# Attention and group norm on one core: two more of eight tiles split, done on GpSimd, with scores four tiles ahead

## The chip, the cores and the metric

The kernel runs on one core of a Trainium2 chip. PE is TensorE, DVE is VectorE, ACT is ScalarE, POOL is GpSimd and SP is SyncE, which only issues DMAs here. The metric is the device time of one launch in microseconds.

## The reference

x is 8 images of 128 channels and 1024 pixels, f32. First an attention for each image, then a normalization over groups of four channels, the partners of each channel being the three that are the least correlated with it over all images.

```python
x_f = jnp.einsum('oc,bcn->bon', Wf, xf) + bf[None, :, None]     # 16 rows
x_g = jnp.einsum('oc,bcn->bon', Wg, xf) + bg[None, :, None]     # 16 rows
x_h = jnp.einsum('oc,bcn->bon', Wh, xf) + bh[None, :, None]     # 128 rows
s = jnp.einsum('bci,bcj->bij', x_f, x_g)
beta = jax.nn.softmax(s, axis=-1)
y = x + gamma[0] * jnp.einsum('bci,bij->bcj', x_h, beta)
x_n = y / jnp.maximum(jnp.linalg.norm(y, axis=2, keepdims=True), 1e-12)
cos = jnp.einsum('bcn,bdn->cd', x_n, x_n) / B
_, idx = jax.lax.top_k(-jnp.abs(cos).T, 4)
# mean and variance of each channel with its three partners, then scale and shift
```

## The kernel before

An image's 1024 pixels i are eight tiles t of 128 rows; all 1024 pixels j lie along the free dimension, in two halves of 512 (a PSUM bank each). All engines run the same list of slots: eight for each image b, one per attend of PE. `run_stages` (L212) writes out images 0, 1, 6 and 7 and loops over 2 to 5; each engine has a `stage` function of its own with what it does in slot t. The order on an engine is the order of its code, and semaphores counted up by each operation tie the engines together.

A tile goes through these steps: `score` (L617, PE) multiplies the parts of f and g into one of two PSUM buffers `s_ps`; `row_max` (L404, DVE) takes the negated maximum of 1024; `exp` (L318, ACT) writes `probs[t]` and the row sums; `invert_sum` (L408, DVE) takes the reciprocal; `scale_values` (L335, ACT) multiplies the tile's values by it; `attend` (L636, PE) adds values times probs onto `o_ps`. Tile t+3 is scored in slot t (AHEAD = 3), which waits for the exponential of tile t+1, since the two share a buffer. In plain f32 a product of 128x128 by 128x512 is two PE instructions. The tiles of SPLIT, 3 and 7, are split instead: `high_part` (L324, ACT) rounds probs to the short format fp32r, `split_parts` (L415 to L421, DVE) makes the rest and the two parts of the values, and three short products take the place of the f32 one. The high part is made in the slot before its low part.

f and g come from one projection (`project_fg`, L606, PE) with both weights four times over, 64 rows each. ACT copies it to SBUF with the bias (`copy_fg`, L308) and makes a negated rounded copy in the rows masked as low parts (L311); the sum of the two is the parts of g (`parts`, L427, DVE) and f (`parts_f`, L266, POOL). This is done in slots 1 to 3 for the image ahead, behind the maxima and exponentials of those slots. The values are projected in slots 5 and 6 (`project_values`, L611) from a copy `x_cur`, and `add_value_bias` (L435, DVE) takes them out of PSUM.

At the image's end `residual` (L447, DVE) writes y; ACT squares it (L348), PE transposes it in the next image (L645) and multiplies it with itself (`gram`, L651); `high_yT` (L362, ACT) and `low_part` (L452, DVE) make the parts for it. POOL makes one over the norm (L282, L289), `scale_gram` (L460, L463, DVE) applies it, `turn_gram` (L657, PE) transposes, `add_gram` (L469, DVE) adds up. All of f, g, values, transposes and gram share one PSUM tensor `w_ps`. DMAs on SP copy x and y to and from `x_cur` and `y_cur`. After the last image come the selection of the partners, the statistics, and scale, shift and store of all images.

## Time and profile before

| | us |
|---|---|
| median of three runs (214.33 to 214.99) | 214.97 |
| span of the profiled execution | 211.9 |
| PE busy | 186.4 |
| DVE busy | 173.7 |
| ACT busy | 143.9 |
| POOL busy | 34.3 |

Busy time is the union of an engine's instructions; they overlap a little at their ends, so what counts for a chain is the distance from one start to the next. The profile is one execution; the time of the runs is some 3 us more than its span. A row of the chain names the engine, the tensor written, the line and how many instructions in a row.

### The profile page before, as it was taken

How to read it: one execution, taken by the hardware profiler on the slowest of the kernel's cores; microseconds unless marked ns; L12 is line 12 of the kernel's file. 1: busy time of each engine (PE TensorE's matmuls, PEld its weight loads, DVE VectorE, ACT ScalarE, POOL GpSimd, SP SyncE). 2: the span in 40 equal slices, each digit the busy share in tenths (PEclk: the TensorE clock that was granted, in tenths of full speed). 3: DMA queues.
4: the chain of work that ended last, by engine and by line, in shares of the span. 5: the costliest groups of instructions: out<-in, count | busy, mean ns of one | idle time of the engine just before them, and what ended most of it. 6: DMA issues, size and time to landing. Idle time of an engine off the chain costs nothing.

```text
span 211.9 us, 2596 instructions
## 1 busy us (share of the span) xinstructions
PE 186.4 (88%) x727; PEld 115.2 (54%) x727; DVE 173.7 (82%) x317; ACT 143.9 (68%) x256; POOL 34.3 (16%) x39
## 2 busy tenths in 40 slices
PE   7669979999999999999999999999999999983100
PEld 3435546465765676466756675657465756462000
DVE  6588989979898889979797979887988898766660
ACT  2548976799379955995499658984799378740320
POOL 0200210034003400160007100520034001001400
PEclk9999999999999999999999999999999999997555
DMA  6240002500060007000520052002200020000198
GB/s 207 89 162 0 0 0 100 203 0 0 39 257 3 0 0 292 6 0 3 205 94 0 0 186 111 0 0 99 99 0 0 3 99 0 0 0 0 53 403 336
DMA packets 4904, 16.16 MB, mean 76 GB/s; under 512 B 544, under 2 KB 672, under 8 KB 4896
## 3 DMA queue, kind: packets, MB, share of 16 engines
q1 hardware_dynamic: 4320, 14.68, 18.4%
q10 hardware_dynamic: 576, 1.38, 1.7%
q8 instruction: 4, 0.07, 0.1%
q14 instruction: 4, 0.03, 0.0%
HBM read 4.52 MB, written 4.19 MB: 41 GB/s over the span
## 4 chain that ended last, share of the span: by engine, by line
PE 71%; DVE 13%; ACT 6%; issue 5%; POOL 1%; DVEq 0%; ACTq 0%; POOLq 0%
PE o_ps L636 40%; PE s_ps L617 11%; PE w_ps L611 6%; PE w_ps L606 6%; DVE nmax L404 3%; PE w_ps L651 3%; ACT probs L318 3%; PE w_ps L645 2%; PE o_ps L603 2%; DVE y_all L596 1%; DVE probs_low L418 1%; DVE g_parts L427 1%; DVE y_cur L447 1%; ACT probs_high L324 1%; DVE values L435 1%
## 5 line engine op out<-in xcount | busy, mean ns | idle before, releaser
L318 ACT ACTIVATE probs<-s_ps,nmax 128x1024 f32<-128x1024 f32 x64 | 70.9, 1108 | 40.5 <-DVE nmax L404 40.5
L636 PE MATMUL o_ps<-probs,vnorm 128*128 128x512 f32 x192 | 90.2, 594 | 0.5 <-DVE y_cur L447 0.5
L404 DVE TENSOR_REDUCE nmax<-s_ps 128x1 f32<-128x1024 f32 x64 | 77.9, 1218 | 10.2 <-PE s_ps L617 9.8
L617 PE MATMUL s_ps<-g_parts,f_parts 128*128 128x512 f32 x128 | 51.6, 485 | 4.6 <-ACT probs L318 2.3
L636 PEld LDWEIGHTS o_ps<-probs,vnorm 128*128 128x128 f32 x192 | 35.3, 189 | 28.8 <-issue 23.2
L266 POOL TENSOR_TENSOR f_parts<-fg,fg_neg 64x512 fp32r<-64x512 f32 x14 | 24.0, 1713 | 122.1 <-ACT fg_neg L311 122.1
L617 PEld LDWEIGHTS s_ps<-g_parts,f_parts 128*128 128x128 f32 x128 | 21.2, 190 | 20.7 <-issue 14.0
L418 DVE TENSOR_TENSOR probs_low<-probs,probs_high 128x1024 fp32r<-128x1024 f32 x16 | 19.5, 1221 | 1.3 <-ACT probs_high L324 1.2
L427 DVE TENSOR_TENSOR g_parts<-fg,fg_neg 64x512 fp32r<-64x512 f32 x16 | 13.9, 871 | 6.6 <-ACT fg_neg L311 6.5
L335 ACT ACTIVATE vnorm<-values,rinv 128x128 f32<-128x128 f32 x48 | 18.8, 391 | 0.0
L611 PEld LDWEIGHTS w_ps<-wd,x_cur 128*128 128x128 f32 x112 | 14.7, 192 | 6.7 <-issue 6.7
L324 ACT ACTIVATE probs_high<-probs 128x1024 fp32r<-128x1024 f32 x16 | 16.8, 1048 | 0.0
L606 PE MATMUL w_ps<-x_all,wd 128*128 128x512 f32 (+1 forms) x32 | 16.7, 615 | 0.0
L611 PE MATMUL w_ps<-wd,x_cur 128*128 128x128 f32 x112 | 14.8, 275 | 0.0
L308 ACT ACTIVATE fg<-w_ps,wd 128x512 f32<-128x512 f32 x16 | 10.8, 676 | 3.2 <-PE w_ps L606 3.2
L636 PE MATMUL o_ps<-probs_high,v_high 128*128 128x512 f32 x32 | 12.7, 398 | 0.1
L636 PE MATMUL o_ps<-probs_high,v_low 128*128 128x512 f32 x32 | 12.6, 394 | 0.0
L636 PE MATMUL o_ps<-probs_low,v_high 128*128 128x512 f32 x32 | 12.5, 391 | 0.0
L318 ACT ACTIVATION_READ_ACCUMULATOR probs<-s_ps,nmax 128x1 f32 x64 | 12.4, 194 | 0.0
L311 ACT ACTIVATE fg_neg<-fg,wd 128x512 fp32r<-128x512 f32 x16 | 11.6, 722 | 0.5
L447 DVE SCALAR_TENSOR_TENSOR y_cur<-o_ps,wd,x_all 128x512 f32<-128x512 f32 x14 | 10.0, 749 | 2.0 <-PE o_ps L636 1.7
L452 DVE TENSOR_TENSOR yT<-w_ps,yT 128x512 fp32r<-128x512 f32 x14 | 9.5, 682 | 2.1 <-ACT yT L362 2.1
(90 smaller groups left out, 165.7 us busy)
## 6 DMA issues: line engine op xcount, KB each, us to landing
x_all<-x_dram SPq DMA_DIRECT2D x7, 512.0 KB, 4.0
x_cur<-x_all SPq DMA_DIRECT2D x7, 512.0 KB, 3.2
y_all<-y_cur SPq DMA_DIRECT2D x7, 512.0 KB, 2.9
out_dram<-y_all SPq DMA_DIRECT2D x5, 512.0 KB, 5.8
out_dram<-y_all ACTq DMA_DIRECT2D x2, 512.0 KB, 4.1
x_all<-x_dram SPq DMA_DIRECT2D x2, 256.0 KB, 3.7
out_dram<-y_all SPq DMA_DIRECT2D x2, 256.0 KB, 2.2
wd<-wide_dram ACTq DMA_DIRECT2D x1, 256.0 KB, 4.3
```

The costliest lines, as they stand in the source:

```text
L266: nc.gpsimd.tensor_tensor(f_parts[b % 2][0:KP, halves[h]], fg32[0:KP, halves[h]], fg_neg[0:KP, halves[h]].bitcast(F32), ALU.add).then_inc( ...
L318: nc.scalar.activation(probs[t][:, :], s_ps[t % 2][:, :], ACT.Exp, bias=nmax[:, t:t + 1], accum_out=rsum[:, t:t + 1]).then_inc(exp_done, 1)
L324: nc.scalar.activation(probs_high[SPLIT.index(t)][:, :], probs[t][:, :], ACT.Copy).then_inc(high_ready, 1)
L335: nc.scalar.activation(vnorm[t][:, :], values[par][:, t, :], ACT.Copy, scale=rinv[:, t:t + 1]).then_inc(vn_ready, 1)
L404: nc.vector.reduce_max(nmax[:, t:t + 1], s_ps[t % 2][:, :], AX_X, negate=True).then_inc(max_ready, 1)
L418: nc.vector.tensor_tensor(probs_low[n][:, :], probs[t][:, :], probs_high[n][:, :].bitcast(F32), ALU.subtract).then_inc(low_ready, 1)
L427: nc.vector.tensor_tensor(to[0:KP, columns], fg32[rows, columns], fg_neg[rows, columns].bitcast(F32), ALU.add).then_inc(done, 1)
L447: nc.vector.scalar_tensor_tensor(y_cur[:, halves[h]], o_ps[:, halves[h]], wd[:, GAMMA:GAMMA + 1], image(x_all, b)[:, halves[h]], ALU.mult, ...
L606: return nc.tensor.matmul(w_ps[:, halves[h]], wd[:, WFG:WFG + P], image(x_all, b)[:, halves[h]], start=True, stop=True)
L611: last = nc.tensor.matmul(to[:, t * P:(t + 1) * P], source[:, t * P:(t + 1) * P], wd[:, WHT:WHT + P], start=True, stop=True)
L617: last = nc.tensor.matmul(s_ps[t % 2][:, h], f_parts[par][:, t * P:(t + 1) * P], g_parts[par][:, h], start=True, stop=True)
L636: last = nc.tensor.matmul(o_ps[:, halves[h]], weights[:, :], rows[:, halves[h]], start=(t == 0 and n == 0), stop=(t == T - 1 and n == len( ...
```

## The change

AHEAD goes from 3 to 4, and SPLIT from (3, 7) to (0, 2, 4, 5). For tiles 0 and 4 ACT makes the high part of the probabilities, already scaled by the reciprocal, and DVE the low one; for tiles 2 and 5 POOL does all: scale, high part, low part. The two parts of the values are no longer scaled and are made by POOL for two tiles at a time, as soon as the value bias is added. The copy of f and g to SBUF goes away: ACT makes the negated rounded copy straight from PSUM, and DVE adds PSUM, bias and that copy for f and g together in one operation of 128 rows; a DMA on SP moves g's 64 rows to the partitions of f (for image 0 DVE writes them there itself). The loop is written out, `x_cur`, `y_cur` and `y_all` and their DMAs go: y is written over x. In slots 0 and 1 the copy and the parts stand ahead of that slot's exponential and maximum. High part and low part of a vector-split tile are in the same slot. The value projections are in slots 4 and 5, the transposes in 2 and 3, the gram in slot 6, its scaling in slot 7 ahead of the residual. The diff, cut to this:

```diff
-AHEAD = 3
-SCALED = 2
-SPLIT = (3, 7)
+AHEAD = 4
+VECTOR_SPLIT = (0, 4)
+POOL_SPLIT = (2, 5)
+SPLIT = (0, 2, 4, 5)
...
+            for b in range(1, B):
+                for h in range(H):
+                    sp.wait_ge(parts_ready, H * b + h + 1)
+                    if b >= 2:
+                        sp.wait_ge(scores, T * (b - 1))
+                    sp.dma_start(g_low[b % 2][0:KP, halves[h]].bitcast(F32),
+                                 fg_parts[b % 2][KP:P, halves[h]].bitcast(F32)).then_inc(g_in[h], 16)
...
+            def split_values(b, h):
+                tiles = SPLIT_VALUES[h]
+                source = values[b % 2][:, tiles, :]
+                pool.wait_ge(v_ready, H * b + h + 1)
+                if b >= 2:
+                    pool.wait_ge(probs_used, T * (b - 1))
+                nc.gpsimd.tensor_copy(v_high[b % 2][:, tiles, :], source).then_inc(vh_ready, 1)
+                pool.wait_ge(vh_ready, H * b + h + 1)
+                nc.gpsimd.tensor_tensor(v_low[b % 2][:, tiles, :], source,
+                                        v_high[b % 2][:, tiles, :].bitcast(F32),
+                                        ALU.subtract).then_inc(vl_ready, 1)
+            def split_probs(b, t):
+                n, count = SPLIT.index(t), pool_split_count(b, t)
+                pool.wait_ge(rinv_ready, T * b + t + 1)
+                nc.gpsimd.tensor_scalar(probs[t][:, :], probs[t][:, :], rinv[:, t:t + 1], 1.0,
+                                        ALU.mult, ALU.mult).then_inc(pool_scaled, 1)
+                pool.wait_ge(pool_scaled, count)
+                nc.gpsimd.tensor_copy(probs_high[n][:, :], probs[t][:, :]).then_inc(pool_high, 1)
+                pool.wait_ge(pool_high, count)
+                nc.gpsimd.tensor_tensor(probs_low[n][:, :], probs[t][:, :], probs_high[n][:, :].bitcast(F32),
+                                        ALU.subtract).then_inc(pool_low, 1)
...
+            for b in range(B):
+                for t in range(T):
+                    its_b, its_t = ahead(b, t + AHEAD - 1)
+                    if b == 0 and t == 0:
+                        split_probs(0, 2)
+                    if its_b < B and its_t in POOL_SPLIT:
+                        split_probs(its_b, its_t)
+                    if t == 4 and b < L:
+                        split_values(b + 1, 0)
+                    if t == 5 and b < L:
+                        split_values(b + 1, 1)
+                    if t == 5 and b > 0:
+                        norm(b - 1)
+            norm(L)
             pool.wait_ge(table_in, 1)
...
+            def negate_high(b, h):
                 act.wait_ge(fg_proj, H * b + h + 1)
-                nc.scalar.activation(fg32[:, halves[h]], w_ps[:, halves[h]], ACT.Identity,
-                                     bias=wd[:, BFG:BFG + 1]).then_inc(fg_copied, 1)
-                act.wait_ge(fg_copied, H * b + h + 1)
-                nc.scalar.activation(fg_neg[:, halves[h]], fg32[:, halves[h]], ACT.Copy,
+                if b > 0:
+                    act.wait_ge(parts_ready, H * (b - 1) + h + 1)
+                nc.scalar.activation(fg_neg[:, halves[h]], w_ps[:, halves[h]], ACT.Identity, bias=bias_neg[:, 0:1],
                                      scale=wd[:, NMASK:NMASK + 1]).then_inc(neg_ready, 1)
...
+            def scale(b, t):
+                if t in POOL_SPLIT:
+                    return
                 act.wait_ge(rinv_ready, T * b + t + 1)
...
+                if t in VECTOR_SPLIT:
+                    nc.scalar.activation(probs_high[SPLIT.index(t)][:, :], probs[t][:, :], ACT.Copy,
+                                         scale=rinv[:, t:t + 1]).then_inc(high_ready, 1)
+                    return
+                act.wait_ge(v_ready, H * b + t // TH + 1)
+                nc.scalar.activation(vnorm[t][:, :], values[b % 2][:, t, :], ACT.Copy,
                                      scale=rinv[:, t:t + 1]).then_inc(vn_ready, 1)
...
+            for b in range(B):
                 for t in range(T):
...
+                    if b < L and t < H:
+                        negate_high(b + 1, t)
+                    nxt = ahead(b, t + AHEAD)
+                    if nxt[0] < B:
+                        exp(*nxt)
+                    nxt = ahead(b, t + AHEAD - 1)
+                    if nxt[0] < B:
+                        scale(*nxt)
+                    if b > 0 and t in (2, 3):
+                        high_yT(b - 1, t - 2)
+                    if b > 0 and t == 4:
+                        square(b - 1)
...
+            def low_part(b, t):
                 n = SPLIT.index(t)
...
+                dve.wait_ge(high_ready, vector_split_count(b, t))
+                nc.vector.scalar_tensor_tensor(probs_low[n][:, :], probs[t][:, :], rinv[:, t:t + 1],
+                                               probs_high[n][:, :].bitcast(F32), ALU.mult,
+                                               ALU.subtract).then_inc(low_ready, 1)
...
+            def parts(b, h):
+                dve.wait_ge(neg_ready, H * b + h + 1)
+                if b >= 2:
+                    dve.wait_ge(scores, T * (b - 1))
+                nc.vector.scalar_tensor_tensor(fg_parts[b % 2][:, halves[h]], w_ps[:, halves[h]], wd[:, BFG:BFG + 1],
+                                               fg_neg[:, halves[h]].bitcast(F32), ALU.add,
+                                               ALU.add).then_inc(parts_ready, 1)
...
+            def residual(b, h):
+                if h == 0:
+                    dve.wait_ge(first_half, b + 1)
+                else:
+                    dve.wait_ge(probs_used, T * (b + 1))
+                nc.vector.scalar_tensor_tensor(x_all[:, b, halves[h]], o_ps[:, halves[h]], wd[:, GAMMA:GAMMA + 1],
+                                               x_all[:, b, halves[h]], ALU.mult, ALU.add,
+                                               accum_out=sums[:, h, b:b + 1]).then_inc(y_ready, 1)
...
+            for b in range(B):
+                for t in range(T):
+                    if t == 0 and b >= 2:
+                        add_gram(b - 2, w_ps[:, BANK:BANK + P])
+                    if t < H and b < L:
+                        parts(b + 1, t)
+                    nxt = ahead(b, t + AHEAD)
+                    if nxt[0] < B:
+                        row_max(*nxt)
+                    nxt = ahead(b, t + AHEAD - 1)
+                    if nxt[0] < B:
+                        invert_sum(*nxt)
+                    if t == T - 1 and b >= 1:
+                        scale_gram(b - 1, w_ps)
+                    if t == T - 1:
+                        residual(b, 0)
+                        residual(b, 1)
+                    if nxt[0] < B and nxt[1] in VECTOR_SPLIT:
+                        low_part(*nxt)
+                    if b >= 1 and t in (3, 4):
+                        low_yT(b - 1, t - 3, w_ps[:, halves[t - 3]])
+                    if b < L and t in (5, 6):
+                        add_value_bias(b + 1, t - 5, w_ps)
+            for h in range(H):
...
+            def score(b, t):
+                if (b, t) != (0, 0) and (b, t) != (0, 1):
+                    pe.wait_ge(exp_done, T * b + t - 1)
+                if b > 0 and t == 0:
+                    for h in range(H):
+                        pe.wait_ge(g_in[h], 16 * b)
...
+            def attend(b, t):
                 if t in SPLIT:
-                    pe.wait_ge(vl_ready, split_count(b, t))
+                    pe.wait_ge(vl_ready, H * b + t // TH + 1)
+                    if t in POOL_SPLIT:
+                        pe.wait_ge(pool_low, pool_split_count(b, t))
+                    else:
+                        pe.wait_ge(low_ready, vector_split_count(b, t))
+                    n = SPLIT.index(t)
+                    high, low = v_high[b % 2][:, t, :], v_low[b % 2][:, t, :]
+                    products = [(high, probs_high[n]), (low, probs_high[n]), (high, probs_low[n])]
                 else:
                     pe.wait_ge(vn_ready, whole_count(b, t))
+                    products = [(vnorm[t][:, :], probs[t])]
...
+                    nxt = ahead(b, t + AHEAD)
+                    if nxt[0] < B:
+                        score(*nxt)
+                    if t == 0 and b < L:
+                        if b == 0:
+                            pe.wait_ge(x_in[1], 16)
+                            pe.wait_ge(parts_ready, H)
+                        else:
+                            pe.wait_ge(x_in[(b + 1) % 2], 16 * ((b + 1) // 2 + (b + 1) % 2))
+                        if b >= 2:
+                            pe.wait_ge(gram_scaled, b - 1)
+                        project_fg(b + 1, 0)
+                    if t == 0 and b >= 2:
+                        pe.wait_ge(v_ready, H * (b + 1))
+                        turn_gram(b - 2, w_ps[:, BANK:BANK + P])
+                    if t == 0 and b == 0:
+                        pe.wait_ge(v_ready, H)
+                    attend(b, t)
+                    if t == 1 and b < L:
+                        if b >= 2:
+                            pe.wait_ge(gram_added, b)
+                        elif b == 1:
+                            pe.wait_ge(v_ready, H * (b + 1))
+                        project_fg(b + 1, 1)
+                    if t in (2, 3) and b >= 1:
+                        h = t - 2
+                        if b < L:
+                            pe.wait_ge(parts_ready, H * (b + 1) + h + 1)
+                        elif h == 0:
+                            pe.wait_ge(gram_scaled, b - 1)
+                        else:
+                            pe.wait_ge(gram_added, b)
+                        transposes(b - 1, h, w_ps[:, halves[h]])
+                    if t in (4, 5) and b < L:
+                        h = t - 4
+                        if b >= 1:
+                            pe.wait_ge(yT_ready, H * (b - 1) + h + 1)
+                        else:
+                            pe.wait_ge(parts_ready, H * (b + 1) + h + 1)
+                        project_values(b + 1, h, w_ps)
+                    if t == 6 and b >= 1:
+                        pe.wait_ge(yT_ready, H * b)
+                        if b < L:
+                            pe.wait_ge(v_ready, H * (b + 1) + 1)
+                        gram(w_ps, range(T)).then_inc(gram_made, 1)
```

## Rows read from the trace of the kernel before

**Rows 1.** Windows, one image: stretch, then busy us of each engine, clock, DMA

```profile
104.23:126.46 22.23, 22.23 (x90) 14.00 (x90) 19.48 (x36) 17.26 (x31) 4.32 (x4) 1.00 0.20 74
```

**Rows 2.** The chain that ended last: start us, us on the chain, what

```profile
6.37 0.69 ACT fg L308
...
37.36 1.95 PE o_ps L636 x4
...
105.98 0.46 PE s_ps L617 x2
106.44 1.72 PE o_ps L636 x4
108.16 0.86 PE w_ps L606 x2
...
112.61 1.39 PE o_ps L636 x6
...
119.23 0.89 PE w_ps L611 x8
...
125.05 0.95 PE w_ps L651 x8
...
188.33 0.45 PE s_ps L645 x4
```

**Rows 3.** Timeline of PE: start us, us, first attend of images 0 and 7

```profile
16.53 1.88 PE L636 MATMUL o_ps<-probs,vnorm 128*128 128x512 f32 x4
...
170.95 1.88 PE L636 MATMUL o_ps<-probs,vnorm 128*128 128x512 f32 x4
```

**Rows 4.** Timeline: how operations follow one another on ACT and DVE

```profile
102.73 1.12 ACT L318 ACTIVATE probs<-s_ps,nmax 128x1024 f32<-128x1024 f32 x1 [1.26 <-DVE nmax L404]
103.74 0.19 ACT L318 ACTIVATION_READ_ACCUMULATOR probs<-s_ps,nmax 128x1 f32 x1
103.83 0.39 ACT L335 ACTIVATE vnorm<-values,rinv 128x128 f32<-128x128 f32 x1
...
106.97 1.21 DVE L404 TENSOR_REDUCE nmax<-s_ps 128x1 f32<-128x1024 f32 x1
108.10 0.15 DVE L408 RECIPROCAL rinv<-rsum 128x1 f32<-128x1 f32 x1
```

**Rows 5.** Groups by line and form: count, busy us, mean ns, idle before, releaser

```profile
L266 POOL TENSOR_TENSOR f_parts<-fg,fg_neg 64x512 fp32r<-64x512 f32 x14 | 24.0, 1713 | 122.1 <-ACT fg_neg L311 122.1
L418 DVE TENSOR_TENSOR probs_low<-probs,probs_high 128x1024 fp32r<-128x1024 f32 x16 | 19.5, 1221 | 1.3 <-ACT probs_high L324 1.2
L324 ACT ACTIVATE probs_high<-probs 128x1024 fp32r<-128x1024 f32 x16 | 16.8, 1048 | 0.0
L308 ACT ACTIVATE fg<-w_ps,wd 128x512 f32<-128x512 f32 x16 | 10.8, 676 | 3.2 <-PE w_ps L606 3.2
L447 DVE SCALAR_TENSOR_TENSOR y_cur<-o_ps,wd,x_all 128x512 f32<-128x512 f32 x14 | 10.0, 749 | 2.0 <-PE o_ps L636 1.7
L435 DVE TENSOR_TENSOR values<-w_ps,wd 128x512 f32<-128x512 f32 x14 | 9.4, 675 | 0.0
L289 POOL TENSOR_TENSOR rnorm<-nsq,mhalf 128x1 f32<-128x1 f32 x8 | 4.5, 568 | 0.7
L463 DVE SCALAR_TENSOR_TENSOR gram_rows<-w_ps,rnorm,gram_high 128x128 f32<-128x128 f32 x7 | 2.5, 351 | 0.2
L282 POOL TENSOR_SCALAR nsq<-stats 128x1 f32<-128x1 f32 x7 | 1.7, 242 | 14.3 <-ACT squares L348 14.3
```

**Rows 6.** Timeline, image 0: POOL's part of f and DVE's part of g

```profile
23.19 1.29 POOL L266 TENSOR_TENSOR f_parts<-fg,fg_neg 64x512 fp32r<-64x512 f32 x1 [12.65 <-ACT fg_neg L311]
...
23.43 1.59 DVE L427 TENSOR_TENSOR g_parts<-fg,fg_neg 64x512 fp32r<-64x512 f32 x1
```

**Rows 7.** DMA issues: count, KB each, median us from issue to landing

```profile
x_cur<-x_all SPq DMA_DIRECT2D x7, 512.0 KB, 3.2
```

**Rows 8.** Windows, ten us of the tail: columns as in group 1

```profile
190.00:200.00 10.00, 3.16 (x16) 2.10 (x16) 6.50 (x27) 1.37 (x3) 2.92 (x5) 0.68 0.00 0
```

430 lines of the change are left out of this document (131 added, 299 removed).

## The prediction

> **What bounds the kernel now.** I read the busy times of one whole image first, then the chain that ended last, then the order of the instructions on each engine. In the image from 104.23 to 126.46 us PE is busy all 22.23 us, VectorE 19.5, ScalarE 17.3, GpSimd 4.3 [rows 1]. So PE sets the pace. The chain agrees: from 37.36 us on it is PE after PE, and its pieces add up to the image [rows 2]: eight scores at 0.46, six plain attends at 1.72, two split attends at 1.39, two f/g projections at 0.86, two value projections at 0.89, two groups of transposes at 0.44, a gram at 0.95 and 0.10 for the turned gram: 22.2. The anchors of the sum are the first attend at 16.53, image 1's at 37.36, the last image's at 170.95, and the last transposes' end at 188.78 [rows 2, 3]. That is 16.5 of head, 20.8 for image 0, 133.6 for six images, 17.8 for the last, and 23.1 of tail to 211.9.
>
> **What the change gives PE.** Two more tiles of eight are split: 2 x (1.72 - 1.39) = 0.66 us less per image, so 21.55 of PE work. That is all PE gains; 8 images would make 5.3 us. It counts only while PE is still the one that is late.
>
> **What it costs to get a tile ready.** Durations as they follow each other on an engine [rows 4, 5]: a maximum takes 1.22 and the next VectorE operation starts after 1.14; an exponential is complete after 1.20 and the next ScalarE operation starts after 1.10; I take 0.05 for a handoff. High part 1.05, low part 1.22 (the new one has a scalar too: 1.22 taken, 1.3 at most), copy from PSUM 0.68, value bias 0.68, residual half 0.75. The new parts operation reads PSUM and SBUF: between the 0.68 of the value bias and the 0.75 of the residual; I take 0.70. Removed from VectorE are four small value operations and the g parts; it stays under 19.5 busy. ScalarE loses two copies and two value scalings and is no bound either. The removed copies of x and y on SP were hidden. The new DMA of g moves 128 KB; the nearest row is 512 KB in 3.2 us [rows 7], its upper end, and the lower is a quarter of that. It starts when the parts are there, and the score that needs it comes 7 us after that, as chain A below shows: hidden. Without that chain's stall the score would come 3.4 us after the parts (4.9 less the copy and the parts), still hidden by 0.2. The DMAs wait behind one another on SP and hold up the load of image b+2, which isn't read until an image later.
>
> **The order inside the queues is the point.** Each engine runs in order, so I write out what a waiting instruction holds up. Count slots t = 0 to 7 of image b, each one attend of PE. The score of slot t is that of tile t+4 and waits for the exponential of tile t+2.
>
> Chain A. PE does the projection of half 1 of the next image after the attend of slot 1. ScalarE in slot 1 has the negated copy ahead of the exponential of tile 5, VectorE has the parts ahead of the maximum of tile 5, though that tile's score was done two operations earlier. Then VectorE's low part of tile 4 waits for ScalarE's high part of tile 4, which stands behind the exponential of tile 5; and the maximum of tile 6 is queued behind that low part. From the end of the projection: handoff 0.10, negated copy 0.73, parts 0.62, maximum 1.27, exponential 1.11, high part 1.10, low part 1.17, maximum 1.27, exponential of tile 6 1.25 = 8.6 us until PE may do the score of slot 4. PE has only slots 2 and 3 in between: (0.46 + 1.39 + 0.44) + (0.46 + 1.72 + 0.44) = 4.9. PE stands 3.7 us per image. In the kernel before, maximum and exponential came ahead of the copies, and the high part was made a slot before its low part was due: there VectorE waited 1.2 us for high parts in the whole run (the idle column of L418 in [rows 5]).
>
> Chain B. From that same exponential on: high yT 0.64, low yT 0.61, maximum of the next image's tile 0 1.27, exponential 1.11, value scaling of tile 7 0.31, squares 1.14, exponential of tile 1 1.11, high part of tile 0 1.10, low part 1.17, value bias 0.61, maximum 1.14, reciprocal 0.08, value bias 0.73; then GpSimd splits these values (0.58 + 0.81, below), norm 0.30 + 0.62, then VectorE scales the gram 0.37 + 0.40, and only then may PE project f and g again. Sum 14.1, less 0.14 by which ScalarE was free before the exponential counted: 14.0. PE's own work over that stretch: 2.74 + 2.74 + 3.13 + 2.18 + 0.46 = 11.25. PE stands another 2.7 us.
>
> An image takes 21.55 + 3.7 + 2.7 = 28.0 us instead of 22.25.
>
> **GpSimd's prices.** No row shows its operations at this size. A two-input one of 64x512 took 1.29 where it began ahead of VectorE's, 1.71 in the mean, and one of 128x1 0.24 [rows 5, 6]. So (1.29 - 0.24)/512 = 2.05 ns per element with two inputs. I take half of that for one input, because two streams are read in the one and one in the other: 128x1024 costs 1.29, 1.29 and 2.34 for the scale, the high and the low part, 4.9 us per tile; 256 elements cost 0.50 and 0.76. The lower end is 0.24 for a one-input and 1.29 for a two-input operation, the upper end 2.34 for each of the three. GpSimd is then busy 2 x 4.9 + 2.5 + 0.9 = 13 us of 28. GpSimd has from the reciprocal in slot t-3 to slot t, 3 slots, less the 1.9 us in which VectorE gets to the reciprocal: 6.6 us (slots 7, 0 and 1), so hidden in the middle images by 1.6 us, and by more where PE stands. In the last image it isn't. The lower end shortens chain B by 0.8 and the last image by 3; the upper end gives 28.4 per image and 2.3 more in the last one. The Trainium skill (GPSIMD Engine Reference, Engine selection) says that elementwise work with one input runs there at roughly line rate, where two inputs take about twice VectorE's time; by its 1.2 GHz a one-input tile would be an estimated 0.85 us, and the whole time some 2 us below mine; no row here shows which.
> The trace shows a collision: VectorE's g parts took 1.59 us when GpSimd had begun 0.24 earlier [rows 6], where the value bias, of as many elements per partition, takes 0.68 [rows 5]. The remaining VectorE operation with two SBUF inputs is the low part; by chain A it runs at slots 1 to 2, when GpSimd is between two tiles, so I put it at nothing; at worst it waits 2.3 us for a GpSimd operation, once per image.
>
> **Head, image 0, last image, tail.** Head: one copy per half and the memsets leave; the first copy from PSUM starts at 6.37 as before [rows 2], and the g and f parts are four operations of 0.67 in a row on VectorE, from 7.1 to 9.8; then maximum, bias, maximum (11.5 to 12.8), exponential, high part, exponential to 16.1, score, projection: first attend at 17.4 (0.9 later). Image 0: both chains run without the gram: 26.3 instead of 20.8 (copies, parts, maxima and exponentials of tiles 3 to 6 from 16.2 to 31.1, PE's slot 4 to 33.9, then maximum, exponential, high part, low part, bias, maximum, bias, maximum, residual to 43.7). Last image: maxima, exponentials and low part up to the reciprocal of tile 5 take 8.3, GpSimd 5.0, then PE 1.39 + 1.72 + 0.95 + 1.88 and the residual 0.9: 20.3 instead of 17.8. Tail: the same steps, 23.1.
>
> **Sum.** 17.4 + 26.3 + 6 x 28.0 + 20.3 + 23.1 = 255.1, against a span of 211.9. Around the span lie 214.97 - 211.9 = 3.1 us, the median of the runs against the profiled one. Forecast 258.2 us.
>
> **Rivals.**
> (a) PE stays the bound, faster: its place is the score of slot 4, and it decides at 4.9 us: if the copies and parts don't hold up the maxima, PE never waits and the time is 214.97 - 5.3 = 209.7. For it: the kernel before has 2.7 us of free VectorE time in each image [rows 1] and the change cuts its operations. Against it: chain A is 8.6 and uses no unknown price. 0.04.
> (b) Chain A alone holds; B hides, because the norm or the value split is earlier than I put it: 25.3 per image and 2 off image 0: 240. For it: B has the many small terms. 0.11.
> (c) GpSimd becomes the bound: at 3 us and more for an operation (by the upper end it isn't yet) the tiles of slots 2 and 5 are late in each image: 265 to 285. For it: 1.71 in the mean where 1.29 was enough [rows 5, 6]. 0.09.
> (d) PE's granted clock falls in the stalls. From 190 to 200 us, where PE was busy 3.2 of 10 us, its mean was 0.68 [rows 8], between the two levels of 1.2 and 2.4 GHz; at half clock for 5 us of work after each stall of chain A it is 7 x 5 = 35 more: 293. Against it: the forecast keeps PE busy three quarters of the time, and its stalls come in pieces of 2 us. The Trainium skill (TensorE: Matmul & The Clock Gate, section HAM oscillation) names repeated waits between bursts of matmuls as what brings half clock, which speaks for this rival; no row here shows it for gaps of this size. 0.03.
> (e) The removed instructions and the new waits cancel: within 0.3%. 0.01.
>
> **Chances and range.** The forecast has 0.72; its bounds are 249 (GpSimd cheap) to 266 (GpSimd dear, low part 1.3, parts 0.75). To leave out no more than 2 in 10 the range takes in (b): 240 to 267. A measurement of this kernel can tell about 0.3% from no change. Faster 0.04, same 0.01, slower 0.95.
>
> **What would show it.** In the changed profile: images 28 us apart; PE busy about 77% in the middle; PE's scores waiting for the exponential, some 3.7 us over slots 3 and 4 (half of it at the score of tile 7, as its exponential is late as well); VectorE's low part waiting for the high part about 1.1 us each time; the maximum of tile 5 starting straight after the parts; the projection waiting for the scaled gram; split attends at 1.39; one-input GpSimd operations near 1.3. It is wrong if scores don't wait, if VectorE's maxima start as soon as the score is there, or if PE waits for GpSimd in the middle images.

## The result and the profile after

The changed kernel took 266.54 us (median of 4 runs, 265.83 to 269.53) beside 214.80 for the kernel before, run in turn with it: a ratio of 1.244, 95% interval 1.237 to 1.250. The forecast was 258.2 with a range of 240 to 267. The time is at the upper edge of the range (the ratio put on the 214.97 that the forecast started from makes it 267.4, just outside); the direction of the loss was right, the centre was 8.3 us too low. Ratios leave out the executions that were over 1.5% longer than the fastest of their kernel: one of the kernel before (259.92 us), and one each of three edited kernels below (277.17, 264.24 and 1085 us).

The page of the profile after, its first rows: busy time of each engine over a span of 264.7 us, the granted clock in 40 slices, and the chain that ended last by engine.

```profile
PE 198.4 (75%) x759; PEld 126.2 (48%) x759; DVE 162.3 (61%) x283; ACT 135.4 (51%) x231; POOL 101.7 (38%) x106
PEclk9858799999999999988999999979999999979655
DVE 31%; PE 27%; ACT 18%; issue 13%; POOL 7%; DVEq 0%; ACTq 0%; POOLq 0%
```

PE, which was busy through the whole image before [rows 1], is busy 75% of the span and makes up only 27% of the chain. VectorE and ScalarE with the time between them ("issue") make up the most. Windows of three neighbouring images and of two short stretches (columns as in group 1):

```profile
75.00:103.30 28.30, 22.75 (x94) 14.68 (x94) 18.90 (x31) 16.23 (x29) 12.14 (x13) 1.00 0.10 28
103.30:133.20 29.90, 24.14 (x94) 16.17 (x94) 18.89 (x31) 16.33 (x29) 12.14 (x13) 0.94 0.10 27
133.20:161.50 28.30, 22.74 (x95) 14.68 (x94) 18.87 (x31) 16.22 (x29) 12.13 (x13) 1.00 0.10 29
...
14.00:20.00 6.00, 5.00 (x9) 2.86 (x10) 3.53 (x7) 4.43 (x8) 2.89 (x3) 0.50 0.00 0
117.00:121.00 4.00, 4.00 (x16) 3.50 (x15) 2.49 (x4) 3.98 (x8) 2.94 (x2) 0.57 0.00 0
```

No engine is full: PE 22.7 of 28.3 us, VectorE 18.9, ScalarE 16.2, GpSimd 12.1. An image that no engine fills is set by the order in which they hand over. The middle image is 1.6 us longer than its neighbours, and its granted clock is 0.94: from 117.5 to about 121 it lay at the lower of its two levels, as it did in the head (the last two rows).

The waits of the whole run (engine and line, what it waited for: us in total, times, longest us):

```profile
DVE probs_low L396 <- ACT probs_high L316: 33.8, 16, 2.2
PE s_ps L593 <- ACT probs L307: 28.6, 18, 2.2
PE w_ps L570 <- DVE gram_rows L444: 5.2, 5, 1.0
PE o_ps L614 <- POOL probs_low L249: 4.2, 6, 3.0
```

VectorE waited 33.8 us for high parts, each time about 2.1, where it was 1.2 us in all before [rows 5]. PE's scores waited for exponentials, its projection for the scaled gram. For GpSimd's tiles PE waited 4.2 us in all: 3.0 of them once, in the last image, and 0.24 before the attend of tile 5 in five others, where the chain ran through ScalarE or VectorE and not through that attend.

Chain A in image 3, read from the chain that ended last (start us, us, what):

```profile
106.84 0.87 PE w_ps L570 x2
...
107.74 0.79 ACT fg_neg L300
...
108.55 0.75 DVE fg_parts L404
109.30 1.14 DVE nmax L387
...
111.67 1.05 ACT probs_high L316
...
112.75 1.28 DVE probs_low L396
114.03 1.15 DVE nmax L387
...
116.46 0.72 PE s_ps L593 x2
```

It is the chain that the prediction wrote out, link by link, from the projection's end at 107.71 to the score at 116.46. The timeline shows the two places where PE stood, and why the second followed the first (start us, us, instruction, in brackets the idle time before it and its releaser):

```profile
109.22 1.21 DVE L387 TENSOR_REDUCE nmax<-s_ps 128x1 f32<-128x1024 f32 x1
110.47 1.11 ACT L307 ACTIVATE probs<-s_ps,nmax 128x1024 f32<-128x1024 f32 x1 [1.95 <-DVE nmax L387]
111.73 0.73 PE L593 MATMUL s_ps<-g_low,fg_parts 128*128 128x512 f32 x2 [1.74 <-ACT probs L307]
112.75 1.28 DVE L396 SCALAR_TENSOR_TENSOR probs_low<-probs,rinv,probs_high 128x1024 fp32r<-128x1024 f32 x1 [2.24 <-ACT probs_high L316]
113.95 1.22 DVE L387 TENSOR_REDUCE nmax<-s_ps 128x1 f32<-128x1024 f32 x1
116.46 0.72 PE L593 MATMUL s_ps<-g_low,fg_parts 128*128 128x512 f32 x2 [1.84 <-ACT probs L307]
```

The maximum at 113.95 is of a tile whose score was ready; it stood behind the low part at 112.75, and that behind the high part at 111.67, and that behind the exponential at 110.47. The anchors, from the same chain: the head up to the first attend of image 0, then the first attends of images 1, 4 and 6 (those of 2, 3, 5 and 7 are at 74.98, 103.30, 161.53 and 219.23), and the attends of tiles 5 and 6 of the last image:

```profile
16.22 1.22 PE s_ps L593 x2
17.44 1.71 PE w_ps L570 x2
19.14 2.56 PE o_ps L614 x6
...
46.61 1.41 PE o_ps L614 x6
...
133.20 1.39 PE o_ps L614 x6
...
191.43 1.39 PE o_ps L614 x6
...
232.28 5.02 PE o_ps L614 x10
```

### The profile page after: what moved, and what is told of

Its sections match the earlier page's. It is cut to its first block, busy times and chain, and to the rows that moved or that the text cites. A ratio compares the mean times of both kernels' runs of the same rounds, so it can differ in the third digit from the quotient of the medians.

```text
span 264.7 us, 2435 instructions
## 1 busy us (share of the span) xinstructions
PE 198.4 (75%) x759; PEld 126.2 (48%) x759; DVE 162.3 (61%) x283; ACT 135.4 (51%) x231; POOL 101.7 (38%) x106
## 4 chain that ended last, share of the span: by engine, by line
DVE 31%; PE 27%; ACT 18%; issue 13%; POOL 7%; DVEq 0%; ACTq 0%; POOLq 0%
PE o_ps L614 13%; DVE nmax L387 12%; DVE probs_low L396 7%; ACT probs_high L316 6%; ACT probs L307 6%; PE w_ps L570 6%; PE s_ps L593 4%; DVE values L418 3%; ACT fg_neg L300 2%; DVE fg_parts L404 2%; POOL v_low L237 2%; ACT squares L325 2%; PE w_ps L575 2%; POOL rnorm L262 2%; PE o_ps L567 1%
## 5 line engine op out<-in xcount | busy, mean ns | idle before, releaser
L593 PE MATMUL s_ps<-g_low,fg_parts 128*128 128x512 f32 x128 | 50.9, 481 | 29.3 <-ACT probs L307 28.6
L614 PE MATMUL o_ps<-probs,vnorm 128*128 128x512 f32 x128 | 62.8, 614 | 0.0
L244 POOL TENSOR_SCALAR probs<-probs,rinv 128x1024 f32<-128x1024 f32 x16 | 18.0, 1123 | 74.3 <-DVE rinv L391 73.8
L593 PEld LDWEIGHTS s_ps<-g_low,fg_parts 128*128 128x128 f32 x128 | 22.3, 200 | 44.5 <-ACT probs L307 37.9
L396 DVE SCALAR_TENSOR_TENSOR probs_low<-probs,rinv,probs_high 128x1024 fp32r<-128x1024 f32 x16 | 20.6, 1285 | 33.8 <-ACT probs_high L316 33.8
L249 POOL TENSOR_TENSOR probs_low<-probs,probs_high 128x1024 fp32r<-128x1024 f32 x16 | 38.1, 2382 | 1.4
L404 DVE SCALAR_TENSOR_TENSOR fg_parts<-w_ps,wd,fg_neg 128x512 fp32r<-128x512 f32 x16 | 12.0, 751 | 23.8 <-ACT fg_neg L300 23.7
L614 PE MATMUL o_ps<-probs_high,v_low 128*128 128x512 f32 x64 | 26.3, 411 | 0.0
L570 PE MATMUL w_ps<-x_all,wd 128*128 128x512 f32 x32 | 17.6, 638 | 5.2 <-DVE gram_rows L444 5.2
L614 PEld LDWEIGHTS o_ps<-probs_high,v_high 128*128 128x128 f32 x64 | 12.5, 196 | 12.1 <-issue 9.7
L316 ACT ACTIVATE probs_high<-probs,rinv 128x1024 fp32r<-128x1024 f32 x16 | 18.2, 1138 | 0.0
L247 POOL CAST probs_high<-probs 128x1024 fp32r<-128x1024 f32 x16 | 16.6, 1041 | 1.0
L575 PEld LDWEIGHTS w_ps<-wd,x_all 128*128 128x128 f32 x112 | 16.4, 210 | 1.4
```

Of the source, the lines that this page charges most:

```text
L244: nc.gpsimd.tensor_scalar(probs[t][:, :], probs[t][:, :], rinv[:, t:t + 1], 1.0, ALU.mult, ALU.mult).then_inc(pool_scaled, 1)
L249: nc.gpsimd.tensor_tensor(probs_low[n][:, :], probs[t][:, :], probs_high[n][:, :].bitcast(F32), ALU.subtract).then_inc(pool_low, 1)
L316: nc.scalar.activation(probs_high[SPLIT.index(t)][:, :], probs[t][:, :], ACT.Copy, scale=rinv[:, t:t + 1]).then_inc(high_ready, 1)
L396: nc.vector.scalar_tensor_tensor(probs_low[n][:, :], probs[t][:, :], rinv[:, t:t + 1], probs_high[n][:, :].bitcast(F32), ALU.mult, ALU.sub ...
L404: nc.vector.scalar_tensor_tensor(fg_parts[b % 2][:, halves[h]], w_ps[:, halves[h]], wd[:, BFG:BFG + 1], fg_neg[:, halves[h]].bitcast(F32), ...
L570: nc.tensor.matmul(w_ps[:, halves[h]], wd[:, WFG:WFG + P], x_all[:, b, halves[h]], start=True, stop=True).then_inc(fg_proj, 1)
```

## The experiments

Theory T (the prediction's): the order inside the queues sets the time. VectorE's low part waits for a high part that ScalarE makes only behind the next exponential, and the next maximum is queued behind it; the copies and parts add their length at the worst moment. Rivals: G, GpSimd's load or its late norm; N, that what the trace shows as clock loss, or some price, carries it; and C, that the place of the copies and parts by itself is the cause. Each ratio below is to the kernel before, run beside it (214.6 to 214.9 us).

**The low part a slot later.** One line of VectorE's order:

```
-                    if nxt[0] < B and nxt[1] in VECTOR_SPLIT:
-                        low_part(*nxt)
+                    due = ahead(b, t + AHEAD - 2)
+                    if due[0] < B and due[1] in VECTOR_SPLIT:
+                        low_part(*due)
```

> The changed kernel, but VectorE makes the low part of tiles 0 and 4 one slot later (slots 6 and 2 in place of 5 and 1), so that the high part is there and the next maximum is not queued behind a wait for it. Theory (queue order, chains A and B): both chains lose the wait for exponential and high part; by the durations of the changed kernel's trace 24.9 us per image in place of 28.3, and 241 us in all. Rival 1 (the copies and parts ahead of the exponentials are the cause, not the high part): under 5 us gained, 262 or more. Rival 2 (GpSimd is the bound): no gain.

Measured: 237.04 us (236.03 to 238.04), ratio 1.104 [1.092, 1.116], 24.92 us per image. The waits of this kernel (columns as above):

```profile
DVE probs_low L396 <- ACT probs_high L316: 6.3, 8, 0.9
PE s_ps L594 <- ACT probs L307: 16.1, 10, 2.2
```

No instruction was removed, only one wait moved behind other work, and 29.5 us went. That is T: the image is as expected (24.9), and the whole is 4 us below the 241 expected, about what the lower clock had cost in images 3, 5 and 7 (below); in this kernel it stays at 1.00 there.

**GpSimd's norm ahead of its value splits.**

```
+                    if t == 4 and b > 0:
+                        norm(b - 1)
                     if t == 4 and b < L:
                         split_values(b + 1, 0)
...
-                    if t == 5 and b > 0:
-                        norm(b - 1)
```

> The changed kernel, but GpSimd makes one over the norm ahead of its two value splits (slot 4) instead of behind them (slot 5). Theory: the end of chain B (value bias, GpSimd's split 1.2 us, norm 0.9 us, scaled gram, projection) is cut by the value split and norm, 1.1 us per image (28.3 to 27.2), 260 us. Rival (b) of the prediction (chain B is covered anyway): no gain, 266.

Measured: 259.26 us, ratio 1.208 [1.200, 1.215], 27.23 us per image. The scaled gram no longer appears among the waits of the projection. So the end of chain B ran through VectorE's value bias, GpSimd's value split and its norm, and was worth 1.1 us per image. So much of G holds: not GpSimd's load, but the place of its norm in the chain.

**Copies and parts behind the exponentials and maxima.**

```
-                    if b < L and t < H:
-                        negate_high(b + 1, t)
                     nxt = ahead(b, t + AHEAD)
                     if nxt[0] < B:
                         exp(*nxt)
+                    if b < L and t < H:
+                        negate_high(b + 1, t)
```

(and in the same way `parts` behind `row_max` on VectorE.)

> The changed kernel, but in slots 0 and 1 the negated copy stands behind the exponential on ScalarE, and the parts behind the maximum on VectorE, as it was in the kernel before. If their place ahead is what costs, as chain A was told, 0.73 + 0.62 us per image go: 258. If the in-order wait for the high part is what costs, the same operations stand in the same cycle, only in another order (the low part then waits for copy and exponential and high part): 28.5 per image, 267.

Measured: two executions, of 266.13 and 277.17 us with mean clocks of 0.92 and 0.87, too far apart for a verdict; the shorter one is near the 267 expected and the 266.54 of the changed kernel. The window of one image of the longer one:

```profile
104.84:135.74 30.90, 25.20 (x94) 16.99 (x94) 18.91 (x32) 16.34 (x28) 12.13 (x13) 0.89 0.09 26
```

In the longer one the clock loss hides the edit's effect. It was repeated below with PE kept at work.

**No tiles on GpSimd, two split tiles of eight.**

```
-POOL_SPLIT = (2, 5)
-SPLIT = (0, 2, 4, 5)
+POOL_SPLIT = ()
+SPLIT = (0, 4)
...
```

(and GpSimd splits the values of these two tiles only.)

> The changed kernel with only tiles 0 and 4 split, tiles 2 and 5 plain f32; GpSimd then has only the value splits and the norm, PE has 0.66 us more work per image, and ScalarE scales two more tiles of values. Theory: neither PE nor GpSimd sets the pace in the middle, so the image stays within 0.5 of 28.3 us, and only the last image gains what it waited for GpSimd (3 us) less the PE work: 265 to 267. Rival (c) (GpSimd is the bound): 10 us or more off.

Measured: 262.04 us (260.95 to 263.12), ratio 1.221 [1.207, 1.234]. An image (columns as in group 1):

```profile
104.32:133.73 29.41, 24.81 (x90) 15.42 (x90) 18.90 (x32) 16.90 (x31) 2.25 (x6) 0.94 0.10 28
```

GpSimd's work falls from 12.1 to 2.3 us, and the image stays as long (28.08 at clock 1.00, this one of 29.41 at 0.94). G falls for the middle. The gain is 3 to 4.5 us, a little more than expected, and most of it lies in the end: from the last projection to the last transposes 48.1 us instead of 51.3, where nothing waits for GpSimd's tile 5 any more.

**PE kept at work in its stall.** Two matmuls more per image, whose results are overwritten by the transposes that follow; nothing that is computed changes.

```
+                        if h == 1:
+                            for _ in range(2):
+                                nc.tensor.matmul(w_ps[:, halves[h]], ident, x_all[:, b - 1, halves[h]],
+                                                 start=True, stop=True)
                         transposes(b - 1, h, w_ps[:, halves[h]])
```

> The changed kernel with two more matmuls of 128x512 f32 on PE in slot 3, ahead of the second transposes: 1.7 us of work whose result is overwritten, in a stretch in which PE stands anyway. Theory (the forecast missed by the clock): the granted clock stays at 1.00 in images 3 and 5, which fall from 29.9 to 28.3 us; with the last image's share the time falls by 3 to 5 us, to 262 or 263, although PE has more to do. Rival (the long images have another cause): no change or up to 2 us more per image.

Measured: 262.14 us (261.22 to 262.69), ratio 1.219 [1.215, 1.223]. The windows of images 3 and 4, and the attends of tiles 5 and 6 of the last image in the chain:

```profile
103.07:131.40 28.33, 24.54 (x98) 15.46 (x98) 18.90 (x32) 16.24 (x28) 12.15 (x13) 1.00 0.10 29
131.40:159.72 28.32, 24.50 (x97) 15.46 (x98) 18.91 (x32) 16.24 (x28) 12.12 (x13) 1.00 0.10 29
```

```profile
230.11 3.34 PE o_ps L614 x10
```

PE did 1.8 us more in each image, the middle images took 28.33, and the kernel became 4.4 us faster. The clock in these stalls cost 4.4 us of the 51.7 lost; with the head and image 0, which this edit does not mend and where the cost is read from rows, N carries a seventh of the loss (7.3 us, below).

**Place of the copies again, with PE kept at work** (the third edit and the fifth together).

> The copies-behind kernel again, with two matmuls of 128x512 in slot 3 of PE (results overwritten) that keep the clock up, to be set against the filled changed kernel (262.1 us, 28.3 per image), which has the same fill. Theory (the wait for the high part in the same slot holds the cycle, not the place of the copies): 28.2 to 28.8 us per image, 261 to 265. Rival (the copies ahead of the exponentials are what costs): 27.0 per image, 253.

Measured: 260.3 us, ratio 1.212 [1.210, 1.215]; 28.24 us per image where the filled kernel takes 28.33 (one image, at a lower clock, took 29.83). C falls for the middle images: with the low part where it is, the copies and parts may stand on either side of the exponentials and maxima. In image 0 their place does count: its score of slot 4 comes at 30.96 us instead of 33.06.

**Parts and value bias moved, the low part left.** PE filled as before; parts behind the maximum, in slots 0 and 2, and the bias in slots 4 and 5.

```
-                    if t < H and b < L:
-                        parts(b + 1, t)
...
+                    if t in (0, 2) and b < L:
+                        parts(b + 1, t // 2)
...
-                    if b < L and t in (5, 6):
-                        add_value_bias(b + 1, t - 5, w_ps)
+                    if b < L and t in (4, 5):
+                        add_value_bias(b + 1, t - 4, w_ps)
```

> The filled changed kernel with two of the three moves of the reordered one: parts behind the maximum in slots 0 and 2, value bias one slot earlier, but the low part left where the change has it. Theory: the low part is the larger share of the 6.2 us: here 26.9 us per image in place of 28.3, 252 us. Rival (parts and bias are the larger share): under 25 per image, 240.

Measured: 252.81 us (251.27 to 253.44), ratio 1.176 [1.171, 1.182], 26.47 us per image:

```profile
100.75:127.22 26.47, 24.17 (x98) 15.43 (x98) 18.44 (x32) 16.24 (x29) 12.17 (x13) 1.00 0.11 31
```

VectorE's wait for high parts even rose, to 46.3 us. 1.9 us per image come from the shorter chains, as expected within 0.5. That is a lower bound of what the two moves are worth: the two added matmuls, which stood off the chain in the filled kernel, stand on it here (chain that ended last):

```profile
112.47 1.98 PE w_ps L686 x4
```

They start only when the parts are there, and the score behind them comes at 114.81, though its exponential was complete at about 113.0; without them the moves may be worth up to 1.8 us more. So this run doesn't show that the low part is the larger share, and which of the two moves brings how much was not separated.

**All three orders at once** (low part a slot later, parts behind the maximum in slots 0 and 2, value bias in slots 4 and 5), without the fill.

> The changed kernel in another order, nothing added or taken away: low parts one slot later; the parts of f and g behind the maximum, in slots 0 and 2 instead of ahead of it in 0 and 1; the value bias one slot earlier, in 4 and 5. Theory: all waits of chains A and B are then shorter than PE's own work, and the image takes the 21.6 to 21.8 us of that work, which is 0.5 less than in the kernel before; with the head's 2.6 us more it is 213.5 us in all. Rival (splitting on GpSimd, the written-out code or the in-place y cost something of their own): 22.5 us per image or more, over 220.

Measured: 217.47 us (216.84 to 218.09), ratio 1.012 [1.009, 1.015]. PE's waits for exponentials are down to 3.5 us, from 28.6. The window of an image:

```profile
84.47:106.55 22.08, 22.03 (x94) 14.67 (x94) 18.94 (x32) 16.09 (x29) 13.92 (x13) 1.00 0.13 37
```

PE is busy 22.03 of 22.08 us again. Everything else of the change is still there: four split tiles, GpSimd, the DMA of g. So 49.1 of the 51.7 us went with the order of three operations, the clock loss of images 3, 5 and 7 among them, since the stalls in which it came are gone. What is left against the kernel before lies at the two ends. Per image it wins 0.17 (22.25 to 22.08), not the 0.66 of the sum: the first projection takes 1.03 instead of 0.86, and the attend of GpSimd's tile 5 takes 1.61 instead of 1.39, together 0.39 of the missing 0.49. That tile's last operation ends at 120.31 where the attend starts at 120.45, since the one before it (a cast, 1.04 elsewhere) took 1.90 beside VectorE's low part, so GpSimd is now just late enough to be felt:

```profile
120.45 1.61 PE o_ps L615 x6
```

```profile
115.93 1.90 POOL L247 CAST probs_high<-probs 128x1024 fp32r<-128x1024 f32 x1
117.92 2.39 POOL L249 TENSOR_TENSOR probs_low<-probs,probs_high 128x1024 fp32r<-128x1024 f32 x1
```

(The first line is of the chain, the others of GpSimd's timeline.) In the last image PE waits through the three operations of GpSimd (chain that ended last, start us, us, what):

```profile
179.16 2.17 POOL probs L244
...
181.38 1.05 POOL probs_high L247
...
182.50 2.38 POOL probs_low L249
...
185.01 3.32 PE o_ps L615 x10
```

**Head and end mended.** The same, with five matmuls to keep PE at work in the head (overwritten, as above), both projections of image 1 in slot 0, its parts in slots 0 and 1, and tile 5 of the last image unsplit.

```
+        def is_split(b, t):
+            return t in SPLIT and not (b == L and t == 5)
...
             for t in range(AHEAD):
+                if t >= 2:
+                    pe.wait_ge(parts_ready, H)
+                    keep_busy(2 if t == 2 else 1)
                 score(0, t)
+            keep_busy(2)
...
                         project_fg(b + 1, 0)
+                        if b == 0:
+                            project_fg(1, 1)
```

> The reordered kernel with its head and its last image mended: PE has five matmuls of 128x512 (results overwritten) in the waits before the first attends, both projections of image 1 stand in slot 0 with their parts in slots 0 and 1, and tile 5 of the last image is plain f32, so that PE doesn't wait for GpSimd there. By the reordered kernel's trace: the half clock of the head costs 1.7 us, the wait for the moved g in image 0 2.1 us, GpSimd's scale, high and low part of tile 5 after the last reciprocal 5.8 us, of which 3.5 can go. 217.5 - 7.3 = 210 us, 2% under the kernel before. Rival: another wait takes the place of each, and it stays at 215 or more.

Measured: 213.54 us, ratio 0.994 [0.992, 0.996]; 3.5 short of what was expected. The larger part is missing in the last image: from its first attend to the end of the last transposes it took 19.07 us in the reordered kernel and takes 17.72 here, so 1.35 of the 3.5 us came. PE doesn't wait for GpSimd there any more, but from 170.85 to 187.06 the chain is PE after PE: most of the wait was covered by work that PE had to do anyway. Head and image 0 gave 2.55 of the 3.8 us (image 1's first attend is at 38.93 instead of 41.48). In image 0 GpSimd is late, in the timeline of VectorE, GpSimd and PE:

```profile
24.84 1.29 DVE L400 SCALAR_TENSOR_TENSOR probs_low<-probs,rinv,probs_high 128x1024 fp32r<-128x1024 f32 x1
```

```profile
24.88 2.16 POOL L248 TENSOR_SCALAR probs<-probs,rinv 128x1024 f32<-128x1024 f32 x1 [1.79 <-DVE rinv L395]
```

```profile
30.74 0.47 PE L623 MATMUL o_ps<-probs_high,v_high 128*128 128x512 f32 x1 [0.49 <-POOL probs_low L253]
```

GpSimd's scale met VectorE's low part and took 2.16 us, its three operations were through at 30.60, and PE had stood 0.49 us for them.

**Tile 5 of image 0 unsplit too.**

```
-            return t in SPLIT and not (b == L and t == 5)
+            return t in SPLIT and not (b in (0, L) and t == 5)
```

> The kernel with head and end mended, and tile 5 of image 0 plain f32 as well: there PE waited for GpSimd's three operations from the reciprocal at 24.88 us to 30.60. Without them the values' scaling is ready about 1 us after the reciprocal; PE's own work up to that attend is 2.9 us longer than the reciprocal, so 2.5 to 3 us of the wait go, less 0.33 for the plain attend: 211 us, 1.7% under the kernel before. Rival: the exponentials of image 0 are as late as GpSimd, and it stays at 213.

Measured: 213.00 us (212.38 to 213.65), ratio 0.993 [0.991, 0.994]. Of the 2.5 us hoped for 0.5 came. More was not to be had there: of GpSimd's 5.7 us PE had stood only the last 0.49 (the line above) and had been at its own work before, and here the chain is PE after PE from 14.01 us to image 1. This version is faster than both kernels, and 0.7% under the kernel before.

**The same fault put into the kernel before.** Its high parts one slot later, behind one more exponential, and nothing else:

```
-                    if (project or t + AHEAD < T) and (t + AHEAD) % T in SPLIT:
-                        high_part(*ahead(b, t + AHEAD, par))
+                    if (project or t + SCALED < T) and (t + SCALED) % T in SPLIT:
+                        high_part(*ahead(b, t + SCALED, par))
```

> The kernel before with one line changed: ScalarE makes the high part of tiles 3 and 7 one slot later, in the slot in which VectorE's low part is due, as the change has it. Theory: VectorE stands for exponential and high part twice per image with the next maximum queued behind; 2.7 us of free VectorE time per image don't cover it: 24.1 us per image in place of 22.25, 228 to 231 us. Rival (VectorE's slack hides it): under 217.

Measured: 226.85 us (226.73 to 227.21), ratio 1.057 [1.055, 1.058], 23.8 us per image instead of 22.25. Its waits:

```profile
DVE probs_low L418 <- ACT probs_high L324: 25.7, 16, 2.2
```

The wait is there (25.7 us instead of 1.2, [rows 5]) and costs 1.55 us per image without any of the rest of the change; the lower end of the expectation was missed by 1 us. So a high part made in the slot in which its low part is due is a cause by itself. In the changed kernel the same fault costs more (28.33 to 24.92, 3.4 us); which part of the change makes it dearer was not shown.

## What the prediction had right, and the step that failed

The mechanism was right: the two chains through the in-order queues set the image's time, with nearly the lengths that were summed. The step that failed is a term of the sum, the loss by PE's granted clock (rival (d)), which the sum had at nothing; it measured 7.3 us. The parts follow.

**The chains.** In image 4, which has no clock loss, an image is 5.64 us from the first projection to the end of the second, 8.7 of chain A and 14.0 of chain B: 28.33. The prediction had 5.39, 8.6 and 14.0. The first projection after a stall takes 1.10 us where 0.86 was taken for it; that is 0.24 of the 0.33, and the rest is chain A. Its links: from one start to the next the copy took 0.81 (0.73 taken), the parts 0.67 (0.62), the maximum 1.25 (1.27), exponential to high part 1.10 (1.11), high part 1.18 (1.10), low part 1.20 (1.17), second maximum 1.25 (1.27), exponential to the score 1.26 (1.25). Three operations cost more than the rows of before from which they were priced, and each carries a scale that its neighbour of before did not: the copy 0.78 us against 0.68, the high part 1.14 against 1.05, the low part 1.285 against 1.22. That the scale is the reason is not shown.

```profile
L316 ACT ACTIVATE probs_high<-probs,rinv 128x1024 fp32r<-128x1024 f32 x16 | 18.2, 1138 | 0.0
L396 DVE SCALAR_TENSOR_TENSOR probs_low<-probs,rinv,probs_high 128x1024 fp32r<-128x1024 f32 x16 | 20.6, 1285 | 33.8 <-ACT probs_high L316 33.8
L244 POOL TENSOR_SCALAR probs<-probs,rinv 128x1024 f32<-128x1024 f32 x16 | 18.0, 1123 | 74.3 <-DVE rinv L391 73.8
L247 POOL CAST probs_high<-probs 128x1024 fp32r<-128x1024 f32 x16 | 16.6, 1041 | 1.0
L249 POOL TENSOR_TENSOR probs_low<-probs,probs_high 128x1024 fp32r<-128x1024 f32 x16 | 38.1, 2382 | 1.4
```

(Groups of the changed kernel: line, engine, operation, shapes, count, busy us, mean ns of one, idle time before and its releaser.)

**The weight given to the copies and parts.** The prediction named two differences from the kernel before: the copies and parts ahead of the maximum, and the high part late. The first alone is worth 0.1 us per image, the second alone 3.4. With the low part where it is, an operation moved off one side of the maximum is paid on the other. As terms of chain A they were right; as a cause to be named first they weren't. Once the low part is a slot later, the place of the parts and the earlier bias together count for 2.8 more: 24.92 to 22.08 (the copies on ScalarE stayed where they were).

**GpSimd.** Its prices were taken from a two-input row and halved: 1.29 for a one-input operation against 1.12 and 1.04 measured, 2.34 for a two-input one against 2.38; 0.50 and 0.76 for 256 elements against 0.40 and 0.73. The tile's three operations take 4.5 us instead of 4.9, and the cover in the middle held but for the 0.24 us at tile 5, off the chain. The Trainium skill (GPSIMD Engine Reference, Engine selection) has one-input work at roughly line rate, an estimated 0.85 us; the two measured rows lie between that and the prediction's price, and the measurement decides. From 256 to 1024 elements the cast goes from 0.40 to 1.04 us, 0.83 ns per element, which is that rate; by these two sizes the other 0.19 us are a fixed part. The wait for g's DMA (2.2 us from issue to landing) stayed hidden too; with the second parts a slot later it does not in image 0, where one wait of PE ended with it: 0.3 us in the reordered kernel, 4.0 in the one with parts and bias moved.

**The centre, 9.6 us of span too low.** 264.7 against 255.1, in its parts:
- Head: first attend at 19.14 instead of 17.4. A score of 1.22 us and projections of 1.71 stand where 0.46 and 0.86 were summed, at a granted clock of 0.50: 1.6 of the 1.7. A score after a stall took 0.73 at full clock, so 0.3 of it is the stall and 1.3 the clock.
- Image 0: 27.47 instead of 26.3. Its first split attend took 2.56 instead of 1.39, again at the lower clock: 1.2.
- Six images: 172.6 instead of 168.0. Images 3 and 5 took 29.90 each, 1.57 more than their neighbours: 3.1 of the 4.6. The rest is the 0.33 per image above, less 0.5 in image 6 (27.80).
- Last image: 22.3 instead of 20.3. The attends of tiles 5 and 6 took 5.02 us, and 3.34 in the filled kernel: 1.7. PE had stood 3.0 us just before them.
- Tail: 23.2, as forecast.

So 7.3 of the 9.6 us are the clock, and the step that failed is rival (d): it was priced as a loss after every stall or none. It came after some: two images of six, the head, the last image. The forecast had it at zero in its own sum, although the head's stalls were in it and the row of the tail showed such a loss [rows 8]. Of the 7.3 us, 4.8 are in images 3, 5 and 7, where the fill took 4.4 us away; the 2.5 of head and image 0 are only read from the rows. Outside the span there were 1.8 us instead of 3.1, which gives back 1.3. The 3.1 was too high from the start: it is the median of the runs less the span of one execution, and in single executions of the kernel before time and span are 2.1 to 2.6 us apart.

**What was said of the changed profile.** Right: images 28 us apart; PE busy 80% (77 forecast); scores waiting 1.74 and 1.84 us, 3.6 of 3.7; the maximum straight after the parts; the projection waiting for the scaled gram; split attends at 1.39. Nearly right: PE's waits for GpSimd in the middle are 0.24 us per image at most and not on the chain. Wrong: the low part's wait of about 1.1 us is 2.1. The 1.1 was the time by which ScalarE is late with the high part alone; VectorE reaches the low part right after its maximum and must sit through the exponential as well, 1.1 more. The sum of chain A had both in it.

**The rivals.** (a) falls: no PE-bound image came before the order was changed. (b) falls: chain B is 14.0 against 11.25 of PE, and moving the norm shortens the image by 1.1. (c) falls with the kernel without GpSimd's tiles. (d) holds with a fifth of its price (7.3 of 35). (e) falls.

## What to carry to other kernels

Before work is taken off the engine that sets the pace, write out the cycle of waits through the in-order queues, with its length beside that engine's work on the same stretch; if the cycle is longer, the saving is worth nothing and the excess is paid every round. A wait that stands in the queue one slot too close to its producer also delays everything behind it: look for the operation that is ready but late, and move the waiting one behind it before touching any price. Then look at the ends of the loop, where no cover exists: a slow engine's share that hides in the middle can be late in the first and the last round. Price such a wait by the time in which the other engine really stands: taking GpSimd's share back gave 1.35 of 3.5 us at the end and 0.5 of 2.5 at the start, since PE had work of its own during the rest.

## What the runs showed of the hardware

**The clock falls in short stalls too.** In image 3 PE stood 1.74 and 1.84 us within 5 us, and was granted the lower level from 117.5 to about 121, while it was busy all the time; its neighbour images, with the same stalls, kept 1.00. Two matmuls more in that stall took the fall away, and the kernel that did more was 4.4 us faster. The Trainium skill (TensorE: Matmul & The Clock Gate, HAM oscillation) names repeated waits between bursts as the cause of such loss; the trace agrees as to the kind, and here the waits were under 2 us and the loss came in two images of six. Why in these was not settled.

**GpSimd beside a VectorE operation with two SBUF inputs.** The scale of 128x1024, 1.12 us in the mean, took 2.16 when VectorE's low part had begun 0.04 earlier. It agrees with [rows 6], with the engines' parts changed over. The Trainium skill (SBUF — State Buffer, Who interferes with whom) has such pairs wait for one another in full; 2.16 is a little less than the 2.4 of the two in a row, so by this one row the two overlapped by some 0.2 us or less. With the low part a slot later the pair met in the middle images as well: low part 1.77 instead of 1.29, cast 1.90 instead of 1.04, which is where that order meets GpSimd. In the changed kernel itself the two did not meet there, as the prediction took it: the means of 1.285 and 1.12 leave no room for it.
